# One attention and mixture-of-experts block on one core: where GpSimd zeroes the third score unit, and how the engines pass a branch that is never taken

## The reference

```python
h = _layernorm(x, axis=-1) * (1 + ca) + sa
x = x + ga * attn(h, wq, wk, wv, wo)     # 16 heads of 16 features
h = _layernorm(x, axis=-1) * (1 + cb) + sb
x = x + gb * ffn(h, router_w, ..., w2, b2)

# in attn: q, k and v keep the largest of every ... features of a head
q = _sparsify_last_dim_topk(proj(wq), feature_keep)
scores = where(causal, -inf, q @ k.T / sqrt(16))
attn = softmax(keep the 64 largest of each row of scores)
out = attn @ v

# in ffn: every expert takes its 512 best tokens
scores = softmax(h @ router_w + router_b)
G, idx = jax.lax.top_k(scores.T, 512)
y = zeros.at[idx].add(G * (relu(toks @ w1 + b1) @ w2 + b2))
```

## Time and profile before

| what | value |
| --- | --- |
| median of three runs | 1017.11 us (1014.6 to 1017.33) |
| time of the profiled execution | 1014.52 us |
| its span | 1012.8 us |
| TensorE busy in matmuls | 840.4 us (83% of the span) |
| VectorE busy | 654.3 us (65%) |
| ScalarE busy | 455.3 us (45%) |
| GpSimd busy | 316.4 us (31%) |
| mean granted TensorE clock | 0.935 |

### The profile page before, as it was taken

The page is one execution under the profiler, slowest core; times in us unless marked ns, Lnnn a source line. Parts: engine busy times, 40 slices in busy tenths (PEclk is TensorE's granted clock), DMA queues, the critical chain, the costliest instruction groups (busy, mean ns, idle before and its releaser), DMA issues. The chain is left out here.

```text
span 1012.8 us, 16388 instructions
## 1 busy us (share of the span) xinstructions
PE 840.4 (83%) x6080; PEld 460.6 (45%) x6080; DVE 654.3 (65%) x1504; ACT 455.3 (45%) x572; POOL 316.4 (31%) x466
## 2 busy tenths in 40 slices
PE   6766999988999979989978978883018999999996
PEld 5542444434444434434434534342014777666664
DVE  6858687678687787696794795544876644544441
ACT  2435667765567746466666567640002111222210
POOL 3612433511533512244332212100005343343222
PEclk9868999999999999999999999996557999999998
DMA  4000000000200001200002102001902443442111
GB/s 146 22 1 1 22 22 1 2 1 2 63 22 1 1 26 60 64 1 1 2 1 86 42 1 86 1 22 68 372 23 65 116 101 65 118 115 32 22 21 21
DMA packets 34852, 46.53 MB, mean 46 GB/s; under 512 B 2184, under 2 KB 30928, under 8 KB 34640
## 3 DMA queue, kind: packets, MB, share of 16 engines
q1 hardware_dynamic: 28624, 36.89, 10.9%
q0 software_dynamic: 6144, 8.52, 5.1%
HBM read 32.69 MB, written 12.72 MB: 45 GB/s over the span
## 5 line engine op out<-in xcount | busy, mean ns | idle before, releaser
L927 ACT ACTIVATE p_buf<-ps 128x1024 f32<-128x1024 f32 x288 | 279.3, 1022 | 168.6 <-PE ps L408 150.8
L768 POOL TENSOR_SCALAR_AFFINE_SELECT p_buf<-p_buf 128x512 f32<-128x512 f32 x128 | 95.7, 772 | 321.1 <-ACT p_buf L927 235.4
L436 PE MATMUL ps<-p_buf,vv 128*17 128x512 f32 (+3 forms) x1664 | 152.3, 467 | 14.4 <-POOL p_buf L768 11.7
L408 PE MATMUL ps<-qx,kd 32*128 32x512 f32 (+3 forms) x1280 | 133.2, 508 | 32.9 <-ACT p_buf L927 13.2
L2089 ACT ACTIVATE h_t<-ps,b_t 128x512 f32<-128x512 f32 x64 | 44.0, 687 | 236.4 <-PE ps L2029 236.4
L1261 DVE SCALAR_TENSOR_TENSOR p_buf<-ps,p_buf 128x1024 f32<-128x1024 f32 x64 | 78.3, 1223 | 91.4 <-PE ps L430 44.5
L2039 PE MATMUL ps<-w_sb,h_t 128*128 128x256 f32 x512 | 112.5, 380 | 0.8 <-ACT h_t L2089 0.8
L2029 PE MATMUL ps<-tok_t,w_sb 128*128 128x512 f32 x256 | 112.6, 598 | 0.0
L2039 PEld LDWEIGHTS ps<-w_sb,h_t 128*128 128x128 f32 x512 | 96.6, 190 | 15.3 <-ACT h_t L2089 1.6
L408 PEld LDWEIGHTS ps<-qx,kd 32*128 32x128 f32 x1280 | 56.2, 187 | 98.3 <-issue 93.7
L352 PE MATMUL ps<-w_t,h_t 128*128 128x512 f32 (+1 forms) x224 | 78.4, 494 | 8.0 <-ACT p_buf L927 4.1
(11 more groups left out here) (288 smaller groups left out, 1241.5 us busy)
## 6 DMA issues: line engine op xcount, KB each, us to landing
w_sb<-in_L_ffn_w_dram SPq DMA_DIRECT2D x16, 1024.0 KB, 8.6
h_table<-xr SPq DMA_DIRECT2D x3, 1056.0 KB, 4.6
x_in<-in_L_attn_x_dram SPq DMA_DIRECT2D x6, 512.0 KB, 4.0
out_dram<-xr SPq DMA_DIRECT2D x3, 1024.0 KB, 5.2
xr<-in_L_attn_x_dram SPq DMA_DIRECT2D x3, 1024.0 KB, 5.7
h_table<-xr SPq DMA_DIRECT2D x2, 528.0 KB, 3.2
xr<-in_L_attn_x_dram SPq DMA_DIRECT2D x2, 512.0 KB, 5.3
p_buf<-in_L_wmod_dram SPq DMA_DIRECT2D x1, 1024.0 KB, 8.7
```

What stands on the lines that cost most here:

```text
L408: m = pe.matmul(o, key, qx[r, par, t0:t0 + w], start=True, stop=not run)
L436: m = pe.matmul(ps[32 * h:32 * h + HD + 1, 6, o:o + w], vv[:, (gi // NG) % 2, i, HG * (gi % NG) + h, :], p_of(gi, u)[:, h, lo:lo + w], sta ...
L768: m = pool.affine_select(p, p, [[0, HG], [1, P]], ALU.is_ge, 0.0, base=0, channel_multiplier=-1)
L927: act.activation(p_of(gi, u)[:, 2 * a:2 * a + 2, :], buf(w), ACT.Exp, scale=0.25).then_inc(free_of(w)[0], 1)
```

## The change

Three things are altered.

1. In GpSimd's list, `tri(gi, 2)` now stands directly behind `tri(gi, 1)`, ahead of `first_rstd(b + 1, 0)` (groups with `g` = 0) and of `keep(b + 1, t0)` (groups with `g` = 1 and 2). In all other groups the order is as before.
2. Every engine loads `bad_f` within its own list in block 1 and keeps it in a register; block 2 has no load. The VectorE instruction that writes `bad_f` raises a semaphore for it, `f_flag`.
3. TensorE and VectorE no longer use `If`. They branch by a `br_ne` over a body with a name, and a hint on this branch stands earlier in block 1: for TensorE ahead of the logits of the last batch's first half, for VectorE ahead of its load. SyncE, GpSimd and ScalarE keep their `If`, without a hint.

```diff
# TensorE, tail of block 1
                 project_o(LAST, 1)
+                ahead["PE"] = pe.mark_branch_hint_location()
                 logits(LAST, (0,))
                 logit_rows(LAST, (0,))
                 turn_h(LAST, 1)
                 flags()
                 logits(LAST, (1,))
                 logit_rows(LAST, (1,))
+                pe.wait_ge(f_flag, 1)
+                general["PE"] = pe.value_load(bad_f[0:1, 0:1])
# SyncE, behind the issue for each half of the last h_table rows
                     sp.dma_start(h_v[LAST][:, ts], xr[:, ts, :]).then_inc(f_hout, 16)
+                    if half == 0:
+                        sp.wait_ge(f_flag, 1)
+                        general["SP"] = sp.value_load(bad_f[0:1, 0:1])
# GpSimd, each group
                     tri(gi, 1)
+                    tri(gi, 2)
                     if g == 0 and pre:
                         first_rstd(b + 1, 0)
                     if tiles:
                         keep(b + 1, t0)
-                    tri(gi, 2)
                     tri(gi, 3)
# GpSimd, end of block 1
                 for hs in halves(LAST):
                     second_rstd(LAST, hs)
+                pool.wait_ge(f_flag, 1)
+                general["POOL"] = pool.value_load(bad_f[0:1, 0:1])
# ScalarE, tail
                 take_logits(LAST, (1,))
+                act.wait_ge(f_flag, 1)
+                general["ACT"] = act.value_load(bad_f[0:1, 0:1])
                 router_exp(LAST, (1,))
# VectorE, flag() and tail
-                    dve.tensor_scalar(bad_f[:, :], good[0:1, 0:1], 5.0 * P, None, ALU.is_lt)
+                    dve.tensor_scalar(bad_f[:, :], good[0:1, 0:1], 5.0 * P, None, ALU.is_lt).then_inc(f_flag, 1)
...
                 router_share(LAST, (0,))
+                dve.wait_ge(f_flag, 1)
+                ahead["DVE"] = dve.mark_branch_hint_location()
+                general["DVE"] = dve.value_load(bad_f[0:1, 0:1])
                 router_max(LAST, (1,))
                 router_share(LAST, (1,))
# block 2, VectorE (TensorE alike, with pe_general and pe_done)
-                general = dve.value_load(bad_f[0:1, 0:1])
-                with dve.If(general == 1):
+                dve.br_ne(general["DVE"], 1, on_true="dve_done", on_false="dve_general").branch_hint(ahead["DVE"])
+                with nc.body("dve_general", valid_engines=[dve.engine]):
...
+                    dve.br("dve_done")
+                nc.switch_bb("dve_done")
                 dve.nop()
```

More of the change, by code:

```diff
@@ L216, in build_kernel @@
         f_pr, f_out, f_var2, f_rstd2 = (sem(n) for n in ("f_pr", "f_out", "f_var2", "f_rstd2"))
+        general = {}
+        ahead = {}
         UNITS = (((1, 128, 384), (3, 384, 128)), ((0, 0, 512),), ((2, 256, 256), (6, 768, 256)), ((4, 512, 512),),
@@ L1553, in _ @@
             def _(sp):
-                general = sp.value_load(bad_f[0:1, 0:1])
-                with sp.If(general == 1):
+                with sp.If(general["SP"] == 1):
                     sp.wait_ge(f_out, 16 * LAST)
@@ L1574, in _ @@
             def _(pool):
-                general = pool.value_load(bad_f[0:1, 0:1])
-                with pool.If(general == 1):
+                with pool.If(general["POOL"] == 1):
                     pool.memset(causal[:, :], 0.0)
@@ L1600, in _ @@
             def _(act):
-                general = act.value_load(bad_f[0:1, 0:1])
-                with act.If(general == 1):
+                with act.If(general["ACT"] == 1):
                     with act.Fori(0, B) as b:
@@ L1639, in _ @@
             def _(pe):
-                general = pe.value_load(bad_f[0:1, 0:1])
-                with pe.If(general == 1):
+                pe.br_ne(general["PE"], 1, on_true="pe_done", on_false="pe_general").branch_hint(ahead["PE"])
+                with nc.body("pe_general", valid_engines=[pe.engine]):
                     with pe.Fori(0, B) as b:
@@ L1738, in _ @@
                         m.then_inc(s_log, 1)
+                    pe.br("pe_done")
+                nc.switch_bb("pe_done")
                 pe.nop()
```

## The result

The changed kernel takes 1012.02 us (median of 8 runs, 1010.88 to 1013.74), the kernel before 1017.63 us (8 runs beside them, 1014.6 to 1019.73). The ratio is 0.9950, with a 95% interval of 0.9936 to 0.9963, so 3.8 to 6.5 us less. The forecast was 1006 with a range of 1002 to 1011: the sign is right, about half of the 10.8 us came, and the median lies 1 us above the range. The profiled execution took 1013.74 us with a span of 1012.0.

The account below looks back on a forecast made before the run. TensorE's waits, on GpSimd's late zeroed squares and at the barrier before block 3, were taken as the bound; attention 7.0 plus hand-over 3.8 gave 10.8 us off 1017.1, so 1006 us, range 1002 to 1011.

Parts of the forecast that it names:

- the stalls come back: Rival, 9%: GpSimd's squares slow VectorE in attention, leaving 3.4 us there, 7.2 with the hand-over, 1010 us.
- gi 0, 3.6 us forecast: First group: the earlier `tri(0, 2)` lets VectorE's mask of unit 4 start 3.6 us sooner; bounds 2.0 and 6.45.
- From there VectorE is busy without a gap to the group's end, and TensorE waits for it: gi 0, after the mask of unit 4: VectorE sets the pace, so the mask's 3.6 us reach the group's end.
- what VectorE itself gains or loses by the new neighbours: Three groups with g = 1: all that may remain of TensorE's 0.77 us stall; 0.15 us each taken, 0.5 in all.
- 0.7 and 0.4 forecast: Gain per group from TensorE's removed stall: 0.7 us in three g = 2 groups, 0.4 in two g = 0 groups.
- the full stall: Groups with g = 0 of batches 1 and 2: upper bound of the gain, TensorE's 0.4 us wait on GpSimd's squares.
- The hand-over, 3.8 forecast: Between the blocks: 4.2 us from loads and far branches, less 0.1 for VectorE's load and 0.3 for `b1_nat`.
- After: branches at 701.6, last to drain is GpSimd: Hand-over: with loads gone and hints working, GpSimd drains last at 702.0 to 702.15 instead of TensorE near 706.3; 4.2 us.
- the hints don't take: Rival, 20%: far targets are still fetched at the branch, only the load's 1.1 us go; 8.0 us in all, 1009.
- the load costs 1.1 us: Hand-over before the change: the flag's load between barrier and branch takes 1.1 us, the far target's fetch 3.2 to 3.4 more.
- it moves as a whole: Block 3: a chain that begins at the barrier, so it shifts by whatever the hand-over gains.
- the slower rivals: Rival "Slower", 3%: `tri(gi, 2)` blocks `keep` or `first_rstd` in all nine groups, costing 20 us against 10.8 won, 9 us slower.

Follow-up runs that it names:

- the zeroing alone: The kernel before with only `tri(gi, 2)` moved ahead of `first_rstd` and `keep`, flag loads and branches as before: 1012.88 us, ratio 0.9952.
- the filler: The changed kernel plus all-zero-weight products on TensorE in gi 0's wait ahead of the transposes: six 1010.20 us (0.9935), three 1010.28 us (0.9932).
- both hints early: The changed kernel with VectorE's hint moved earlier and 70, 80 or 26 instructions added to TensorE's stream: 1012.11, 1014.70 and 1010.25 us.
- the loads alone: The kernel before with each engine's `bad_f` load moved into its own block 1 list, plain `If`, no hints, old `tri` order: 1017.66 us, ratio 0.9998.
- the loads and hints alone: The kernel before with the `bad_f` loads moved into block 1 and both hints, old `tri` order: 1016.18 us, ratio 0.9989.
- the short store: The kernel before with the `bad_f` loads moved, no hints, and the last `h_table` store cut to a quarter; read for the hand-over alone, 4.2 us.

## Why the prediction was off

**Sum and sign.** By the traces 3.05 us came from attention and 1.0 from the hand-over, 4.0 in all, inside the measured 3.8 to 6.5 but at its lower end; the difference to the medians' 5.6 isn't traced. The forecast had 7.0 and 3.8. Its rival "the stalls come back" had 3.4 for attention, close to the 3.05, but from other terms: 2.0 for gi 0 and nothing lost in g = 1. That it came near is luck.

**gi 0, 3.6 us forecast, 0.85 came.** Failed step: "From there VectorE is busy without a gap to the group's end, and TensorE waits for it". What stands ahead of it held: the mask moved by 3.48. The sentence itself was not quite so even before the change, where VectorE waits 0.31 us ahead of `lw` and 1.15 us for TensorE ahead of `neg_in`. And I had not asked what a shorter stall here does to the one behind it. TensorE now waits 3.19 us for the next mask instead of 1.65, in nine of ten executions its clock falls to 0.50, and the work behind that wait takes 1.8 times as long. VectorE then waits for TensorE (with the zeroing alone at `lw`, 2.54 us instead of 0.31). In the kernel before the clock was at 0.50 as well, from 85 to 92 us, but in and behind the long stall; it was back at 1.00 when the mask of unit 4 started, and the rest of the group ran at full speed. Where the clock stays at 1.00, by the filler or without it, the 3.5 us are there.

**g = 1, +0.15 forecast, -0.43 came, three times.** Failed step: the sign of "what VectorE itself gains or loses by the new neighbours". The bounds, 0 and 0.77, left a loss out without a reason, although the price of two neighbours was in the earlier trace rows. The scan, which I had counted on to have fewer squares beside it, takes 2.60 us before and after. VectorE lost 0.27 at the first `y_one`, which a wait of 0.26 behind it took up, and 0.75 at `k_not`, and won 0.31 at the second `y_one`: 0.44 us. `k_not` is the larger part, and it doesn't just run slower beside a neighbour. In the 138 cases of the 18 profiles in which it starts while GpSimd is within a multiplication or a copy, it ends 0.55 us after that instruction's end, and so takes 0.72 to 1.64 us; in the 100 cases with GpSimd idle it takes 0.68, and so it does when GpSimd's instruction starts just behind it. The change moved the start of the multiplication to just ahead of `k_not` in g = 1 (in gi 6, with g = 2, to 0.04 us behind it, and there `k_not` takes 0.68). Putting the old order back in these groups returned the loss.

**g = 2 and g = 0.** 0.7 and 0.4 forecast, 0.75 and 0.62 to 0.63 came. Right in mechanism and, for g = 2, in size. In g = 0 more came than "the full stall" that was to be the upper bound; of the further 0.2, TensorE's wait for `xr` gives 0.1 (0.97 instead of 1.08 us), behind a `k_not` of 0.68 instead of 0.80; the other 0.1 wasn't followed.

**The hand-over, 3.8 forecast, 1.0 came.** Two steps failed. "After: branches at 701.6, last to drain is GpSimd" supposed that both hints are in force wherever they stand. The rival "the hints don't take" is what the total showed, for VectorE fully and for TensorE by half (1.63 us in one execution, since the packet came only at 700.13, and 4.47 in another with the same stream, where none came). But its reason was not that hints do nothing: moved ahead, they do all that the forecast said (hand-over 1.1 us). The Trainium skill (Runtime: NRT & Kernel Launch, Instruction fetch mechanics) has the prefetch purely sequential, by which an early hint would gain nothing; the runs with both hints early show otherwise, 0.39 and 0.49 us instead of 3.45. Second, "the load costs 1.1 us" when it leaves the barrier: with the loads alone the hand-over shrinks by only 0.3 (5.18 to 4.84) and the time not at all, since the fetch of the far branches then waits for the last store of `h_table`. The load had been covered by that transfer, and I had looked for the store's effect on `b_nat` alone. A third thing that the forecast took for granted, "it moves as a whole" of block 3, doesn't hold where the hand-over is short: block 3 was 306.3 us before, 306.9 in the changed kernel, and 307.8 to 308.6 with both hints in force.

**What held.** VectorE's load was not in the way of `router_max`; the slower rivals did not come; `b_nat` costs 0.2 to 0.6 us where the hand-over ends early, forecast 0.3.

**What stays open.** The exact rule by which a hint becomes a fetch. Also why two executions with the same stream of TensorE, in the changed kernel and with the loads and hints alone, differ in whether the packet came before the branch. It is so without hints too: with the loads alone none came between 673 us and the branch, and with the short store, whose TensorE stream is the same, one came at 697.83. And why the clock fell in gi 0 in nine executions and not in the tenth.

## What to carry to other kernels

When a stall is removed, follow the engine to its next wait and ask whether that wait gets longer and what clock it leaves behind: here a wait of 3.2 us instead of 1.7 cost 2.7 us in gi 0, and three products of no use won them back there. A hint or a prefetch is worth what lies between it and the branch in its own stream, so look for the instruction packet between the two, not for microseconds of lead. Then see whether the stretch behind keeps its length: of 3.1 us won at the hand-over about half was lost in block 3. And when a cost leaves a hand-over, check which transfer it had been hiding: the branch's own fetch can be that transfer.

## What the runs showed of the hardware

- A far branch's instruction packets start about 1.0 us after the branch when the store is short or nearly done, and 1.8 to 2.1 us after it when 528 packets of a store are under way; TensorE's branch, when no packet came ahead of it, then takes 3.45 to 3.67 or 4.2 to 4.5 us. It ends 1.3 to 1.5 us after its packet has landed.
- An instruction of TensorE that only waits on a semaphore already met takes 106 ns (80 in 8.7 us), so instructions added to move a boundary are not free.
- With unchanged code TensorE's granted clock scatters in three places: 1.00 or down to 0.50 from 68 to 76 us (some 2.7 us in the first group: 39.28 and 41.93 in two kernels whose first group is the same), 28.50 or 30.14 us for gi 14, and in block 3, where it comes back from 0.50 after 64 to 68 us and up to 1.9 us go with that. By an estimate from these three this is most of the 5 us by which executions of one kernel differ, and it is why the lengths of single groups told these changes apart where the totals could not.
- What VectorE's `k_not` pays for GpSimd depends on which of the two starts first: `k_not` (128x1024) started within a GpSimd multiplication or copy ends 0.55 us after it (138 cases, up to 1.64 us), against 0.68 us alone or when it starts first. In the other direction, the first zeroing beside VectorE's scan takes 2.35 us instead of 0.63.
